# FFN phase of a perceiver layer, written without loops: each tile's down products laid between the next tile's gate and up products

## What is computed

```python
x = x + xattn(layernorm(x), ctx_2048, ...)
x = x + attn(layernorm(x), W_Q, b_Q, W_K, b_K, W_V, b_V, W_O, b_O)      # its sum over heads is the merge phase
x = x + ffn(layernorm(x), gate_up_packed, gate_up_scales, down_packed, down_scales)

def ffn(x, ...):                       # x: 2048 tokens x 512
    w_gu = dequant_fp4(gate_up_packed, gate_up_scales, 128)    # 2816 x 512, one scale for 128 inputs
    w_down = dequant_fp4(down_packed, down_scales, 128)        # 512 x 1408
    gate, up = split(x @ w_gu.T)
    y = (silu(gate) * up) @ w_down.T
    return y / sqrt(mean(y * y) + 1e-6)
```

## Time and profile before

| | |
|---|---|
| time, median of 3 | 1392.92 us (1392.2 to 1392.96) |
| time of the profiled execution | 1399.19 us |
| its span | 1397.4 us |
| mean granted clock of TensorE | 0.989 |
| busy share: PE, DVE, ACT, POOL | 96%, 72%, 36%, 27% |

### The profile page before, as it was taken

The page is one execution under the profiler, slowest core; times in us unless marked ns, Lnnn a source line. Parts: engine busy times, 40 slices in busy tenths (PEclk is TensorE's granted clock), DMA queues, the critical chain, the costliest instruction groups (busy, mean ns, idle before and its releaser), DMA issues. The chain is left out here.

```text
span 1397.4 us, 24040 instructions
## 1 busy us (share of the span) xinstructions
PE 1344.6 (96%) x9220; PEld 776.4 (56%) x9220; DVE 1006.3 (72%) x2309; ACT 507.1 (36%) x1249; POOL 375.9 (27%) x302
## 2 busy tenths in 40 slices
PE   8999999967999999999999999999899999999998
PEld 6666666534666666666666666654344434343433
DVE  6444444247888888888888887838899696969693
ACT  3222222222343333433343334320001665748281
POOL 0000000003222222222222222203033482919192
PEclk9999999989999999999999999999999999999999
DMA  8555555522101111111201021376841000000000
GB/s 333 211 197 199 202 192 189 214 83 87 31 31 31 44 45 50 31 31 61 61 31 31 16 61 31 91 190 193 187 162 61 1 1 30 0 30 0 30 1 30
DMA packets 36927, 122.47 MB, mean 88 GB/s; under 512 B 4313, under 2 KB 4953, under 8 KB 28121
## 3 DMA queue, kind: packets, MB, share of 16 engines
q1 hardware_dynamic: 36552, 118.19, 25.4%
q10 hardware_dynamic: 272, 2.88, 0.9%
HBM read 95.89 MB, written 25.17 MB: 87 GB/s over the span
## 5 line engine op out<-in xcount | busy, mean ns | idle before, releaser
L871 POOL TENSOR_TENSOR hd_rotated<-hd_products 64x512 f32<-64x512 f32 x32 | 40.3, 1259 | 741.0 <-DVE hd_products L1123 741.0
L191 PE MATMUL psum<-hd_xt_hi,hqk_hi 128*128 128x512 f16 x512 | 194.6, 380 | 1.6 <-DVE hd_xt_lo L1097 1.6
L192 PE MATMUL psum<-hd_xt_lo,hqk_hi 128*128 128x512 f16 x512 | 194.3, 379 | 0.0
L193 PE MATMUL psum<-hd_xt_hi,hqk_lo 128*128 128x512 f16 x512 | 194.3, 379 | 0.0
L1480 POOL TENSOR_TENSOR ff_part<-ff_part 128x512 f32<-128x512 f32 x88 | 127.8, 1468 | 103.9 <-DVE ff_part L1607 103.5
L191 PE MATMUL psum<-hd_wv_hi,hd_xt_hi 128*128 128x256 f16 x512 | 140.3, 274 | 4.2 <-DVE hd_wv_lo L1102 4.2
L1509 PE MATMUL psum<-ff_xt_hi,gu 128*128 128x512 f16 x352 | 133.9, 380 | 9.0 <-DVE w_rows L1645 3.3
L192 PE MATMUL psum<-hd_wv_lo,hd_xt_hi 128*128 128x256 f16 x512 | 140.4, 274 | 0.0
L193 PE MATMUL psum<-hd_wv_hi,hd_xt_lo 128*128 128x256 f16 x512 | 140.3, 274 | 0.0
L1510 PE MATMUL psum<-ff_xt_lo,gu 128*128 128x512 f16 x352 | 133.4, 379 | 0.0
L1607 DVE SCALAR_TENSOR_TENSOR ff_part<-psum,gu_scale,ff_part 128x512 f32<-128x512 f32 x176 | 119.8, 738 | 6.3 <-ACT ff_part L1557 3.6
(11 more groups left out here) (181 smaller groups left out, 3007.1 us busy)
## 6 DMA issues: line engine op xcount, KB each, us to landing
xa_kv_t<-in_ctx_t_dram SPq DMA_DIRECT2D x16, 1024.0 KB, 5.7
xa_kv<-in_ctx_dram SPq DMA_DIRECT2D x16, 1024.0 KB, 4.8
w_rows<-in_head_weights_dram SPq DMA_DIRECT2D x12, 1024.0 KB, 8.0
z_scratch<-hd_z_hi SPq DMA_DIRECT2D x32, 256.0 KB, 2.6
z_scratch<-hd_z_lo SPq DMA_DIRECT2D x32, 256.0 KB, 3.3
w_rows<-z_scratch SPq DMA_DIRECT2D x8, 1024.0 KB, 8.9
hqk_lo<-z_scratch SPq DMA_DIRECT2D x8, 1024.0 KB, 8.4
xn<-in_x_dram SPq DMA_DIRECT2D x8, 512.0 KB, 3.9
```

What stands on the lines that cost most here:

```text
L191: pe.matmul(out, lh, rh, start=(first and i == 0), stop=False)
L192: pe.matmul(out, lh, rl, start=False, stop=False)
L193: last = pe.matmul(out, ll, rh, start=False, stop=(final and i == k - 1))
```

## The change

The FFN's loops are gone, every instruction of the four tiles is written out. Down work is cut into 44 jobs a tile, a job being the three matmuls of one hidden block for one token block. Behind the last group of tile t's gate and up stand three jobs of tile t, the turn of tile t+1 and six more jobs of tile t; the other 35 are laid between the groups of tile t+1, one or none after every two (`beside`). The last tile's jobs run at the end by themselves.

For this, `h_hi` and `h_lo` have a second pair of buffers (in `wo_hi`, `wo_lo`), the results too. From tile 1 on, the groups turn round six banks (`ROUND`), and the down products have two, 4 and 5. A finished down block of tiles 0 to 2 is squared by ScalarE and also copied out of PSUM by it (`square`); VectorE makes one root chain for all four blocks, in two parts (`root_start`, `root_end`), two tiles later, and finishes the rows from SBUF (`finish`). That of tile 2 and of the last tile comes after the last unit; the last tile's is cut in three. Layernorm statistics and scaling of the next tile become side work of VectorE after certain units (`side_work`): for tile 1 the scaling stands in tile 0, and its statistics in the merge phase, ahead of the last two `add`. The four `warm` transposes are gone, and the first group that reads a slice of `xt` waits for that slice alone.

In the loads, x1 of tile 1 comes after the second code words of the merge phase, and x1 of tile 3 one tile later, ahead of the down weights.

```diff
@@ heads_phase, load_for_merge
-                for t in range(2):
-                    sp.dma_start(early.x2[:, t * TT:(t + 1) * TT, :], rows_of(t * TILE)).then_inc(early_sems.x1_loaded, 16)
+                sp.dma_start(early.x2[:, 0:TT, :], rows_of(0)).then_inc(early_sems.x1_loaded, 16)
@@ merge_phase, SP
             sp.dma_start(codes[1], codes_of(gu_codes, 1)).then_inc(gu_loaded[1], 16)
+            load_x1(1)
             for t in range(1, NT - 1):
                 sp.wait_ge(z_used[1], t)
                 load_z(t, 1)
                 if t == 2:
+                    load_x1(3)
                     load_down()
...
                 if t == 1:
                     load_x1(2)
-                    load_x1(3)
@@ merge_phase, VectorE
+                if b == NT * TT - 3:
+                    dve.wait_ge(added, 2 * TT)
+                    layernorm(dve, 1, x2[:, TT:2 * TT, :], xn, stat, ln_step, xn_ready, parts=(1, 2, 3, 4))
@@ ffn_phase
+        FIRST, SECOND = 3, 9
+        jobs = [(0, b) for b in range(SECOND)] + [(1, b) for b in range(3)] + [(0, b) for b in range(SECOND, FB)] + \
+            [(1, b) for b in range(3, FB)] + [(i, b) for i in (2, 3) for b in range(FB)]
+        beside = [jobs[SECOND:][n * (len(jobs) - SECOND) // (2 * UNITS):(n + 1) * (len(jobs) - SECOND) // (2 * UNITS)] for n in range(2 * UNITS)]
...
+        ROUND, RESULTS = (6, 7, 0, 1, 2, 3), (4, 5)
...
+        placed = [(unit, n % 8) for n, unit in enumerate(tile_0)] + [(unit, ROUND[n % len(ROUND)]) for n, unit in enumerate(in_order)]
+        placed += [(("y", t, i), RESULTS[i % 2]) for t in range(NT - 1) for i in range(TT)]
@@ ffn_phase, TensorE
+            def gate_up(t, u, g):
+                first = u % 2 * FF + u // 2 * P
+                unit = ("p", t, u, g)
+                if u == 0:
+                    banks.wait_moved(pe, None, ("x", t, g))
+                banks.wait_room(pe, None, unit)
...
+            for t in range(NT - 1):
+                for i, b in jobs[0:FIRST]:
+                    down(t, i, b)
+                turn_xn(t + 1)
+                for i, b in jobs[FIRST:SECOND]:
+                    down(t, i, b)
                 for u in range(UNITS):
+                    for half in range(2):
+                        for g in (2 * half, 2 * half + 1):
+                            gate_up(t + 1, u, g)
+                        for i, b in beside[2 * u + half]:
+                            down(t, i, b)
+            for i, b in jobs:
+                down(NT - 1, i, b)
@@ ffn_phase, ScalarE
+            def square(t, i):
+                unit = ("y", t, i)
                 banks.wait_filled(act, None, unit)
...
+                act.activation(junk[:, :], psum_of(unit), ACT.Square, accum_out=squares[:, t % 2, i:i + 1]).then_inc(squares_done, 1)
+                if t < NT - 1:
+                    if t >= 2:
+                        act.wait_ge(out_stored[t % 2], 16)
+                    banks.moves(act.activation(results[t % 2][:, i, :], psum_of(unit), ACT.Copy), None, unit)
@@ ffn_phase, VectorE
+            def root_start(t, first, end):
+                at = slice(first, end)
+                dve.wait_ge(squares_done, t * TT + end)
+                done(dve.tensor_scalar(rms["var"][:, at], squares[:, t % 2, at], 1.0 / D, RMS_EPS, ALU.mult, ALU.add))
+                inverse_root(dve, {k: v[:, at] for k, v in rms.items()}, done, rounds=1)
...
+            def finish(t, i):
+                to = results[t % 2][:, i, :]
+                from_ = to
...
+                dve.scalar_tensor_tensor(to, from_, rms["y"][:, i:i + 1], x2[:, t * TT + i, :], ALU.mult, ALU.add).then_inc(finished, 1)
+
+            def side_work(t, u):
+                if t == 0:
+                    if u in (4, 8, 12, 16):
+                        scale_block(1, u // 4 - 1)
+                    return
+                if t < NT - 1:
+                    if u in (0, 2, 4, 6):
+                        statistics(t + 1, (u // 2 + 1,))
+                    if u in (8, 10, 12, 14):
+                        scale_block(t + 1, u // 2 - 4)
+                if t >= 2:
+                    if u == 5:
+                        root_start(t - 2, 0, TT)
+                    if u == 7:
+                        root_end(0, TT)
+                    if u in (9, 11, 13, 15):
+                        finish(t - 2, (u - 9) // 2)
+
+            second_halves(0)
+            for t in range(NT):
                 for b in range(FB + 1):
+                    for u in (2 * b, 2 * b + 1) if b < FB else ():
+                        scale_and_add(t, u)
+                        side_work(t, u)
+                    if b == FB and t < NT - 1:
+                        second_halves(t + 1)
                     if b:
+                        gated(t, b - 1)
+            for t, first, end in ((NT - 2, 0, TT), (NT - 1, 0, 2), (NT - 1, 2, 3), (NT - 1, 3, 4)):
+                root_start(t, first, end)
+                root_end(first, end)
+                for i in range(first, end):
+                    finish(t, i)
```

More of the change, by code:

```diff
@@ L1533, in _ @@
-            with nc.tensor.Fori(0, NT - 1) as t:
-                tile(t, False)
-            tile(NT - 1, True)
+                        last = pe.transpose(psum_of(unit)[:, block_of(i)], xn[:, i, block_of(k)], ident[:, :])
+                    banks.fills(last, None, unit)
+            def gate_up(t, u, g):
[3 more added lines that the diff above has]
+                    banks.wait_moved(pe, None, ("x", t, g))
+                banks.wait_room(pe, None, unit)
+                pe.matmul(psum_of(unit), gu[:, g, first:first + P], xt_hi[:, g, :], start=True, stop=False)
+                banks.fills(pe.matmul(psum_of(unit), gu[:, g, first:first + P], xt_lo[:, g, :], start=False, stop=True), None, unit)
@@ new lines, in down @@
+            def down(t, i, b):
+                unit = ("y", t, i)
+                h_hi, h_lo = h_pairs[t % 2]
+                if b == 0:
+                    banks.wait_room(pe, None, unit)
+                if i == 0:
+                    pe.wait_ge(h_lo_done, t * FB + b + 1)
+                last = three_passes(pe, psum_of(unit), [(h_hi[:, b, block_of(i)], h_lo[:, b, block_of(i)])],
+                                    [(down_hi[:, b, :], down_lo[:, b, :])], first=(b == 0), final=(b == FB - 1))
+                if b == FB - 1:
+                    banks.fills(last, None, unit)
@@ L1584, in tile @@
-                act.wait_ge(squares_done, t * TT + TT)
-                act.nop(nofuse=True)
-            with nc.scalar.Fori(0, NT - 1) as t:
-                tile(t, False)
-            tile(NT - 1, True)
+                        hidden_hi(t, b - 2)
+                    if b == FB and t < NT - 1:
+                        first_halves(t + 1)
+                    for i in range(TT - 1):
+                        if t and unit_after(i) in (2 * b - 1, 2 * b):
+                            square(t - 1, i)
@@ L1591, in _, with second_halves @@
+                if t:
+                    square(t - 1, TT - 1)
+            for i in range(TT):
+                square(NT - 1, i)
         @block.vector
         def _(dve):
[L1593 removed]
+            def second_halves(t):
                 for k in range(KD):
[L1595 to L1598 removed]
@@ L1649, in _, with scale_and_add @@
-            tile(0, True, False)
-            with nc.vector.Fori(1, NT - 1) as t:
-                tile(t, False, False)
-            tile(NT - 1, False, True)
+                    unit = ("x", t, k)
+                    dve.wait_ge(xt_hi_done, t * KD + k + 1)
+                    banks.moves(dve.tensor_tensor(xt_lo[:, k, :], psum_of(unit), xt_hi[:, k, :], ALU.subtract), None, unit)
+            def scale_and_add(t, u):
+                for g in (2, 3):
+                    unit = ("p", t, u, g)
+                    banks.wait_filled(dve, None, unit)
+                    banks.wait_moved(dve, None, ("p", t, u, g - 2))
+                    to = part[:, slot_of(t, u), g - 2, :]
+                    banks.moves(dve.scalar_tensor_tensor(to, psum_of(unit), scale_of(u, g), to, ALU.mult, ALU.add), None, unit)
```

255 lines of the change are left out of this document (110 added, 145 removed).

## The result

| | median (runs) | ratio to before, 95% interval |
|---|---|---|
| before | 1394.26 us (1391.54 to 1406.48, 20) | |
| after | 1387.26 us (1377.65 to 1396.56, 20) | 0.9942 [0.9921, 0.9962] |

The ratio makes it 8.1 us faster, 5.3 to 11.0 by its interval. I had said 17.2 less, 1375.7 us and 1366 to 1386: the direction was right, the size was not. The profiled execution took 1384.99 us, with a span of 1383.2.

What follows compares the result with a forecast made beforehand. GpSimd and VectorE together were taken to bound gate and up, TensorE down, with a z stall before the FFN. Terms -16.7 + 5 - 1.5 - 4 = -17.2 us gave 1375.7 us, range 1366 to 1386.

Steps and rivals of the forecast that it cites:

- the loads: Merge phase: reordering x1's loads shortens TensorE's wait for z; -4 us, between nothing and 7.9.
- The sign that I had named for this term: Merge phase: TensorE's wait for z near 980 us would be between 1 and 4 us.
- The condition that I had put on the term: End of merge phase: the gain holds only if VectorE keeps up; added statistics hold up to 2 us if TensorE came 8 earlier.
- The weave: FFN, three periods: down jobs laid between gate and up groups let TensorE set the pace, 68.2 us each; -16.7 us.
- The chains: Mainly FFN tile 2: VectorE's layernorm and root chains wait for GpSimd; +4 us, plus 1 for tile changes.
- another 1.4: Tile 2: VectorE's further lateness over four pairs of units with scaling and result, after 7.8 us late; 1.4 us.
- Rival C: Whole change: every chain part pays its whole bound and the z wait stays; -8.2 us, 1384.7 us, chance 0.28.
- B: Whole change: no chain waits for GpSimd and both z waits go; -26.1 us, 1366.8 us, chance 0.18.
- the late h_lo: Last tile: an h_lo can come late for job 13; 1 us, counted only in the bound.
- Tile 0: First FFN tile: earlier start -1.4, no wait for the first down bank -1.1, four scalings +1; sum -1.5 us.
- The end: Last tile's down, root, result and store stand as before, earlier roots hidden by TensorE's down; 0 us.
- E: Tiles 1 to 3: VectorE's two-input instructions each wait for GpSimd, a loss; up to 1412 us, chance 0.04.

Runs made afterwards that it cites:

- weave only: The changed kernel with the x1 loads in their old order, against the kernel before: 1383.98 us, 0.9896.
- after again: The changed kernel, unchanged, measured a second time against the kernel before: 1385.15 us, 0.9914.
- early scaling: The changed kernel with the four scalings of tile 1's rows after units 0 to 3 of tile 0: 1385.89 us in one execution.
- codes behind z: The changed kernel with the third and fourth groups' code words on SyncE's queue behind z, not on ScalarE's: 1380.02 us, 0.9893 against the kernel before.
- tiny scaling: The changed kernel with tile 1's four scalings cut to 4 elements, output invalid: first FFN stretch 46.1 us instead of 47.9, one execution.

## Why the prediction was off

**The step that failed** is the loads: "I take half, -4, because a wait that gets shorter may spare the clock." Alone they gave 1.0002 with the wait still there, and with the code words out of the way again nothing (0.9960 against 0.9959). The argument had a wrong reading in it: "the queue is busy all the time (DMA share 0.86 to 0.95)". Those rows are of 980 to 990 us, when the wait had begun and the next loads were being issued; from 970 to 980 the share was 0.53. I bounded the term by the whole wait without asking what else was under way between the issue and the landing, and that was ScalarE's load of code words. What the whole wait is worth was measured as well, by moving these: 5.7 us timed (2.1 to 9.4) and 8.5 in the trace, near the 7.9 of the bound.

The sign that I had named for this term came true by luck: the wait was 3.2 us in the first trace, between 1 and 4. The same kernel again had 4.3, and weave only, with the old loads, 1.9.

The condition that I had put on the term was right: the added statistics "would hold up to 2 us if TensorE came 8 earlier". Where z came early they held 1.4 to 1.9.

**The weave** was right: -16.7 was counted on 68.2 us a period, and tile 1 takes 68.22. Three periods fell by 10.7 where -11.7 was booked.

**The chains** were right in mechanism and nearly in size (its "another 1.4" should be 1.6 by the figures beside it): 4 + 1 booked, 5.8 measured in tile 2, next to nothing in tiles 1 and 3. Of the 5.8, 4.1 are in every execution with early roots (72.3 - 68.2); the other 1.7 is the clock, which the prediction didn't have. It was half for some 3 us after the 2.2 us wait in "after", "after again" and "early scaling", and stayed full after the same wait in "weave only", "codes behind z" and "tiny scaling". Rival C, which paid the whole bound (7.3), was too high, B too low. C's sum, -8.2, is all but the -8.1 of the first timing, and that is in part luck: the z wait did stay, but the chains cost 6.0 and not 7.3, tile 0 gave -0.3 and not +0.2, and the late h_lo at 1 us didn't come; the second timing gave -12.0.

**Tile 0** was booked at -1.5 and gave -0.3 (from the first transpose to the first down product it was 1140.50 - 1094.21 = 46.29 us, now 1136.91 - 1090.91 = 46.00). The start did come 2.0 us sooner and the 1.14 us wait went; but that stretch is paced by VectorE, and there the scalings took 1.9 and not 1. Without them it would have gained 2.2 and not 3.1, so 0.9 us of the earlier start went into waits later in the stretch. The prediction had taken 0.68 us each from the place after the last unit, where GpSimd is idle. In the median one takes 1.38.

**The end** was booked at 0: from the last tile's down to the end of the span 35.6 us before and 35.7 now.

**The sum** by these measured terms is -10.7 - 0.3 + 0.1 + 0 = -10.9 for the FFN, and nothing for the loads. Of the 6.3 us from there to the forecast of -17.2, the loads are 4.0, tile 0 is 1.2, the chains with their clock 1.0 and the end 0.1. The two timed ratios make it -8.1 (5.3 to 11.0) and -12.0 (8.1 to 15.9). E, the slower case, did not come up: a chain part waited for one or two GpSimd instructions, 0.9 to 2.0 us, as the argument against it said.

**Open.** Why the later transfer of z takes 22.3 to 29.0 us with the words beside it, and so the wait 1.9 to 8.3. It was 5.3, 6.3 and 8.3 in the three executions with loops and 1.9 to 5.4 in the six with the weave, whatever the order of the loads; I have no mechanism by which the FFN's code could reach back there, and three against six is no proof.

## What to carry to other kernels

When a transfer is late, list every queue that has something under way between its issue and its landing before you reorder the queue it stands in: here z took about twice as long beside the second queue's load, and the order of the first queue was worth nothing that could be told. Look at the share of the engines in that time itself, not after it. When side work moves onto an engine beside a busy neighbour, take its duration from rows beside that neighbour, not from where it stood idle. Two dependent chains of tiny instructions in the same few units cost 4 us, and up to 1.7 more by the clock; apart they cost 0.7: spread them, but not up to the last product of the tile.

## What the runs showed of the hardware

- A VectorE instruction on 4 elements a partition waits for the whole GpSimd instruction under way: L127 takes 1.12 us instead of 0.17. It has a single SBUF input. The scaling too has one tensor input in SBUF, and takes 0.74 us alone and up to 1.50 beside GpSimd. The Trainium skill's page "SBUF — State Buffer", section "Who interferes with whom", says that `tensor_scalar` can enter a two-port mode and then contends; that it contends agrees with these rows. That it runs in such a mode they don't show: alone the scaling is no faster (0.74 us) than the product with two inputs (0.68). In the prediction I took an instruction with a single SBUF input for safe, and so let the scalings off.
- TensorE's granted clock fell to its lower level (1.2 GHz) for some 3 us after a wait of 2.2 us in the middle of dense work, in three executions, and in three others with the same wait it didn't. At the start of the FFN it was at that level after a gap of 2.4 and of 2.9 us, and at the upper one after a gap of 2.8. The windows of "after" around it, in which a full one holds 25 matmuls in 5 us:

```profile
1240.00:1243.50 3.50, 1.34 (x7) 0.39 (x4) 3.36 (x7) 1.20 (x3) 1.69 (x2) 1.00 0.00 0
1243.50:1246.00 2.50, 2.40 (x7) 0.78 (x8) 2.50 (x4) 2.21 (x5) 1.65 (x1) 0.71 0.00 0
1246.00:1250.00 4.00, 4.00 (x15) 1.64 (x14) 4.00 (x6) 1.44 (x3) 3.73 (x3) 0.76 0.00 0
1250.00:1255.00 5.00, 5.00 (x25) 2.28 (x24) 4.47 (x7) 3.17 (x6) 4.06 (x3) 1.00 0.01 2
```
